# Attention over 1024-token windows: three score banks, three maxima banks, and a later place for the value matmuls

## The reference, cut to what matters

```python
x = x + _L0_conv_ref(_gn(x), L0_conv_weight)
x = x + _L1_conv_ref(_gn(x), Wr, Wqkv, Wp, bp, W1, b1, W2, b2)

def _dmha(x, Wr, Wqkv, Wp, bp):                  # inside _L1_conv_ref, x: [16, 4096 tokens, 288]
    xr = x @ Wr.T
    C2 = xr.shape[-1]                            # 144
    hd = C2 // NUM_HEADS                         # 8 heads of 18
    qkv = (xr @ Wqkv.T).reshape(B, N, 3, NUM_HEADS, hd).transpose(2, 0, 3, 1, 4)
    n = N // N_CHUNKS                            # 4 chunks of 1024 tokens
    ...
    attn = jnp.einsum('bhcnd,bhcmd->bhcnm', q, k) * scale
    attn = jax.nn.softmax(attn, axis=-1)
    o = jnp.einsum('bhcnm,bhcmd->bhcnd', attn, v)
    o = o.transpose(0, 2, 3, 1, 4).reshape(B, N, C2)
    return o @ Wp.T + bp
```

## Time and profile before

| | |
|---|---|
| median of 3 runs | 13767.46 us (13765.76 to 13772.49) |
| profiled execution, its span | 13760.1 us |
| attention phase in it | about 4479 to 12953 us |
| PE busy over the span | 93% |
| DVE busy | 71% |
| ACT busy | 57% |
| POOL busy | 20% |
| mean granted TensorE clock | 0.969 of full speed |

### The profile page before, as it was taken

One profiled execution on the slowest core, in us unless ns is written; L12 is line 12 of the kernel. 1 busy time (PEld: TensorE's weight loads), 2 busy tenths in 40 slices (PEclk: granted clock), 3 DMA queues, 4 the chain that ended last, 5 costly groups with the idle time before them and its releaser, 6 DMA issues. The chain is left out here.

```text
span 13760.1 us, 258672 instructions
## 1 busy us (share of the span) xinstructions
PE 12819.6 (93%) x76348; PEld 5285.8 (38%) x76348; DVE 9806.3 (71%) x18034; ACT 7890.2 (57%) x14774; POOL 2684.0 (20%) x2692
## 2 busy tenths in 40 slices
PE   6999999999993799999999999999999999999899
PEld 3545544544552233333333333333333333333233
DVE  7888888888886676777777777777777777677411
ACT  4666666666663365666665666666666666566511
POOL 3445444444441000000000000000000000000144
PEclk9999999999996799999999999999999999999999
DMA  2110110101104222222222232222222222222254
GB/s 73 21 21 15 21 20 16 21 15 21 21 15 134 67 61 67 65 62 63 67 65 63 61 71 63 60 68 66 61 62 66 67 63 61 66 63 64 62 127 105
DMA packets 853449, 773.62 MB, mean 56 GB/s; under 512 B 587076, under 2 KB 621348, under 8 KB 840740
## 3 DMA queue, kind: packets, MB, share of 16 engines
q1 hardware_dynamic: 850468, 747.29, 24.0%
q10 hardware_dynamic: 1536, 8.39, 0.3%
HBM read 510.50 MB, written 244.96 MB: 55 GB/s over the span
## 5 line engine op out<-in xcount | busy, mean ns | idle before, releaser
L1495 DVE TENSOR_REDUCE a_big<-a_mp 128x1 f32<-128x512 f32 x8192 | 5225.0, 685 | 2325.0 <-PE a_mp L1328 2060.3
L1414 ACT ACTIVATE a_ex<-a_sc 128x512 f32<-128x512 f32 x8192 | 4450.3, 599 | 2366.1 <-PE a_sc L1316 2121.6
L1328 PE MATMUL a_mp<-a_ks,a_qs 108*128 108x512 bf16 x8192 | 3188.5, 389 | 188.5 <-DVE a_big L1495 86.1
L1316 PE MATMUL a_sc<-a_qs,a_ks 111*128 111x512 bf16 x8192 | 3157.0, 387 | 125.3 <-issue 80.6
L849 DVE TENSOR_TENSOR r_prod<-r_pg,r_win 128x512 f32<-128x512 f32 x3584 | 2318.9, 683 | 533.1 <-PE r_pg L583 279.6
L1342 PE MATMUL a_po<-a_ex,a_va 128*32 128x512 f32 x16384 | 2221.0, 615 | 18.6 <-ACT a_ex L1414 17.8
L1230 POOL TENSOR_TENSOR a_pieces<-a_left,a_pieces 128x512 bf16<-128x512 f32 x256 | 295.4, 1154 | 7904.8 <-ACT a_pieces L1400 7904.8
L1316 PEld LDWEIGHTS a_sc<-a_qs,a_ks 111*128 111x128 bf16 x8192 | 797.2, 98 | 2529.3 <-ACT a_ex L1414 1807.7
L524 POOL TENSOR_TENSOR r_prod<-r_temp,r_win 128x512 f32<-128x512 f32 x1024 | 1214.8, 1207 | 1401.8 <-PE r_pl L632 621.3
L1328 PEld LDWEIGHTS a_mp<-a_ks,a_qs 108*128 108x128 bf16 x8192 | 802.3, 98 | 1598.8 <-DVE a_big L1495 1009.9
L587 PE MATMUL r_pg<-r_ident,r_spread 128*128 128x128 f32 x9216 | 1195.7, 278 | 112.0 <-DVE r_prod L849 93.3
(11 more groups left out here) (192 smaller groups left out, 11692.5 us busy)
## 6 DMA issues: line engine op xcount, KB each, us to landing
a_qs<-qk_parts SPq DMA_DIRECT2D x768, 144.0 KB
a_ks<-qk_parts SPq DMA_DIRECT2D x768, 144.0 KB
qk_parts<-a_pieces SPq DMA_DIRECT2D x128, 768.0 KB, 5.0
f_t<-mixed SPq DMA_DIRECT2D x48, 1536.0 KB, 16.4
a_tw<-second SPq DMA_DIRECT2D x512, 128.0 KB, 3.0
mixed<-a_t SPq DMA_DIRECT2D x256, 256.0 KB, 2.1
r_win<-first SPq DMA_DIRECT2D x128, 280.5 KB, 5.2
a_zw<-layered SPq DMA_DIRECT2D x192, 144.0 KB, 11.8
```

The lines of the kernel that those rows point to most:

```text
L1316: pe.matmul(sc[x][:, :], ks[0:KROWS + NPART, p.h, head, 128 * kb:128 * kb + 128], qs[0:KROWS + NPART, p.h, head, CHUNK * qb:CHUNK * qb + C ...
L1328: pe.matmul(mp[half][:, :], qs[0:KROWS, p.h, head, 128 * q:128 * q + 128], ks[0:KROWS, p.h, head, CHUNK * half:CHUNK * half + CHUNK], star ...
L1414: nc.scalar.activation(ex[:, k % RING, :], sc[x][:, :], ACT.Exp, scale=scale).then_inc(exped.sem, 1)
L1495: nc.vector.tensor_reduce(big[:, x % 2, k // 2:k // 2 + 1], mp[x % 2][:, :], AX_X, ALU.max).then_inc(maxed.sem, 1)
```

## The change

The eight PSUM banks are dealt out anew: three for scores, three for maxima, one each for `po` and `pm`. Tile k of a unit, scores and maxima alike, uses bank k % 3 of its kind. A unit has 128 tiles, which is not a multiple of three, so `bank_before` works out which earlier tile used the bank last, within the unit or at the end of the unit before. The value matmuls of the step before move by one tile: they now stand after the third score and maximum of a step. On ACT, `outputs` moves behind all four exponentials of its step.

```diff
+BANKS = 3
+PER_UNIT = QUAD * STEPS
+
+
+def bank_before(k):
+
+    if k >= BANKS:
+        return k - BANKS + 1
+    return max(j for j in range(PER_UNIT - BANKS, PER_UNIT) if j % BANKS == k % BANKS) - PER_UNIT + 1
...
-    sc = [ctx.enter_context(nc.psum_tensor(f"a_sc{i}", [128, CHUNK], F32)) for i in range(QUAD)]
-    mp = [ctx.enter_context(nc.psum_tensor(f"a_mp{i}", [128, CHUNK], F32)) for i in range(2)]
+    sc = [ctx.enter_context(nc.psum_tensor(f"a_sc{i}", [128, CHUNK], F32)) for i in range(BANKS)]
+    mp = [ctx.enter_context(nc.psum_tensor(f"a_mp{i}", [128, CHUNK], F32)) for i in range(BANKS)]
...
-            if not (isinstance(p.n, int) and p.n == 0 and k < QUAD):
-                pe.wait_ge(exped.sem, exped.at(p.n, k - QUAD + 1))
-            pe.matmul(sc[x][:, :], ks[0:KROWS + NPART, p.h, head, 128 * kb:128 * kb + 128],
+            if not (isinstance(p.n, int) and p.n == 0 and k < BANKS):
+                pe.wait_ge(exped.sem, exped.at(p.n, bank_before(k)))
+            pe.matmul(sc[k % BANKS][:, :], ks[0:KROWS + NPART, p.h, head, 128 * kb:128 * kb + 128],
...
-            pe.wait_ge(maxed.sem, maxed.at(p.n, k - 1))
-            pe.matmul(mp[half][:, :], qs[0:KROWS, p.h, head, 128 * q:128 * q + 128],
+            pe.wait_ge(maxed.sem, maxed.at(p.n, bank_before(k)))
+            pe.matmul(mp[k % BANKS][:, :], qs[0:KROWS, p.h, head, 128 * q:128 * q + 128],
...
-                    if x == 1 and t == 0 and -1 in which:
+                    if x == 2 and t == 0 and -1 in which:
                         values(p.to(-1), STEPS - 1)
-                    elif x == 1 and t and 0 in which:
+                    elif x == 2 and t and 0 in which:
                         values(p, t - 1)
...
-                nc.scalar.activation(ex[:, k % RING, :], sc[x][:, :], ACT.Exp, scale=scale).then_inc(exped.sem, 1)
+                nc.scalar.activation(ex[:, k % RING, :], sc[k % BANKS][:, :], ACT.Exp, scale=scale).then_inc(exped.sem, 1)
...
                 if 0 in which:
                     exponentials(p, t, 0)
+                    exponentials(p, t, 1)
                 if t == 0 and -1 in which:
                     outputs(p.to(-1), 3)
                 elif t and t % 8 == 0 and 0 in which:
                     outputs(p, t // 8 - 1)
-                if 0 in which:
-                    exponentials(p, t, 1)
...
-            nc.vector.tensor_reduce(big[:, x % 2, k // 2:k // 2 + 1], mp[x % 2][:, :],
+            nc.vector.tensor_reduce(big[:, x % 2, k // 2:k // 2 + 1], mp[k % BANKS][:, :],
```

## The result

| | before | changed |
|---|---|---|
| median | 13769.37 us (4 runs, 13765.76 to 13772.49) | 13452.02 us (4 runs, 13439.59 to 13459.34) |
| ratio, 95% interval | | 0.9768 (0.9754 to 0.9781) |
| span of the profiled execution | 13760.1 us | 13457.6 us |

The change makes the kernel 317 us faster. The forecast was 284 us faster, 13483 us, in a range of 13435 to 13590. A control of the same kernel beside the experiments gave 13443.08 against 13763.5, 320 us less.

The account below looks back on a forecast made before the run. PE was taken as the bound, with maximum matmuls waiting for reductions to free their banks. Terms -267 - 17 + 13 - 4 - 9 = -284 us, from 13767.5 to 13483 us; 8-of-10 range 13435 to 13590.

Parts of the forecast that it names:

- steps 2 to 31 of 62 units, waits of the maxima: Attention steps where maxima wait for a bank: 4.3 us saved per unit in 62 units, -267 us.
- steps 0 and 1 of 33 units that no return precedes: Unit starts that are no loop start: 0.52 us saved at each of 33, -17 us.
- unit -1: Unit with maxima only, at half clock: 2.4 in place of 2.8 in 19 steps, plus three projection steps, -9 us.
- unit 63: Unit with scores only: values come 0.17 us sooner in some 25 steps, -4 us.
- The third maxima bank: Steps without a task: maxima no longer wait for reductions, so each step loses its 0.46 us excess and runs at 2.85.
- The margins of 0.15 and 0.24: Fed steps: the tightest maximum finds its bank free 0.15 us early, the tightest score 0.24 us early.
- the rival of half the gain: Fourth reduction comes 0.35 us later, nine steps a unit keep 0.2 to 0.25 of waiting: 13611 us, chance 0.10.
- The third maxima bank, with the later place of the values: Heading of the -267 us term, which costed the extra bank and the moved value matmuls as one item.
- One score bank less costs nothing in the steady steps: Steady steps: each score finds its bank free, 0 us; if the cover went, each 0.1 us would cost 56 us.
- Loop starts: Starts of 29 loop rounds: PE stops earlier with three score banks, 0.45 us each, +13 us, bounds 0 and 29.
- the clock's rival: Lower clock for longer at loop starts, or in the steps themselves, makes the kernel slower: chance 0.05.
- The engines did not slow each other: Answers the no-change rival: unpaused engines slow each other, reductions stretch from 0.60 to 0.8, near 13767 us; chance 0.04.
- the 250 us more: Extra gain if matmuls of fed steps stood about 131 ns apart, as the Trainium skill says, not 0.22 us.

Follow-up runs that it names:

- banks alone: Changed kernel with the value matmuls and the copy of `po` put back to their old place, three and three banks kept: 13459.23 us, ratio 0.9781.
- the score bank alone: Kernel before with three score banks in place of four, two maxima banks, eighth bank unused, old place of the values: 13773.19 us, ratio 1.0003.
- the two loops of twelve: Twelve units per loop round in place of two: changed kernel 13187.48 us, ratio 0.9579; kernel before 13507.73 us, ratio 0.9810.
- the place alone: Changed kernel's order (values behind the third tile, `po` copy behind all exponentials) with the old four score and two maxima banks: 14136.24 us, ratio 1.0269.

## Why the prediction was right, by its own steps

The sum of the prediction was -284 us, the two profiled executions differ by -302.5. Read off their traces, unit by unit:

| step of the prediction | forecast | in the trace |
|---|---|---|
| steps 2 to 31 of 62 units, waits of the maxima | -267 | -269.4 |
| steps 0 and 1 of 33 units that no return precedes | -17 | -19.8 |
| steps 0 and 1 behind the 29 returns | +13 | +13.7 (control: +1.9) |
| PE's gap at the return itself | 0 | -7.4 |
| unit 0 | 0 | -7.1 |
| unit -1 | -9 | -13.3 (control: -10.5) |
| unit 63 | -4 | -3.9 |
| other phases | 0 | +4.5 |

**The third maxima bank** was right in mechanism and size. Steps 20 to 24, 30 and 31 took 2.85. Steps 14 and 25, which the prediction also put at 2.85, have a task of their own and took 5.05 and 3.28, but they lost the same 0.46 and 0.47. The margins of 0.15 and 0.24 held, and the rival of half the gain falls with them.

**"The third maxima bank, with the later place of the values"** was a false pairing. The place gives nothing in the steady steps (banks alone: 2.84 too); it trims 16 us, mostly at the edges of units. With two banks it costs 2.7%. That the pairing did no harm to the number is luck: the same count with the old place gives 2.85 as well.

**One score bank less costs nothing in the steady steps**: right (the score bank alone). The next one would cost 791 us.

**Loop starts**: the mechanism is seen in the trace (PE stops at step 0's fourth score, one piece of 5.12 us). The size lies between 0 and 14 us and is not settled: one trace says 13.7, the control 1.9, the score bank alone 11.6, and the medians of the two loops of twelve nothing. Behind the 29 returns of one trace these two steps together vary with a standard deviation of 1.0 to 1.5 us, from which I estimate a chance error of about 10 us for such a difference of two traces. That +13.7 stands so near +13 is therefore luck.

**What was missed.** Unit 0 runs the steady form with nine such steps of its own; I left it out of the 62 and gave it nothing, and it saved 7.1. PE's gap at the return shrank from 2.94 to 2.69 us on average; it is 2.69 with the banks alone too, and 2.83 with the place alone and with the score bank alone, and no experiment says why. Unit -1 ran its steps at 2.39 as forecast, and gained 2 to 4 us more, most of it in the steps with tasks, whose lengths differ between the traces of one kernel. Lastly, the median moved by 317 and the profiled executions by 302: the span of the profiled run of before lies 9 us under the median, that of the changed kernel 6 us over. I had set the forecast by the first offset alone. Single executions of this kernel differ by up to 23 us, and those of before by up to 27; the control's span, 325 us shorter, lies 8 us under its median.

**A slip in the description.** The kernel's loop covers units 2 to 61 in 30 rounds with 29 returns, and units 0 and 1 are written out before it. The text ahead of the prediction says units 4 to 61 in 29 rounds. The count of 29 slow starts, units 4 to 60, is right, as is every term that uses it.

**The other rivals.** The granted clock of unit 21 stayed at 1.00, and the mean of the profiled run is 0.969 as before, so neither form of the clock's rival came. From unit 0 to unit 62 both traces have the lower level behind returns alone, 11.3 us of it for each before, and 10.5 (control: 11.3) after. The engines did not slow each other either: reductions take 685 ns in both pages, and three in a row still follow each other at (1.89 - 0.69)/2 = 0.60 us. Score and maximum matmuls stand 0.22 us apart in the fed steps too, the pace that the sum kept; the 250 us more, estimated from a closer one, did not come.

## What to carry to other kernels

When two engines share buffers in a ring, and the producer has a stretch in which it makes nothing for the consumer, the ring must hold what the consumer can eat in that stretch and after, and this shows as waits of the producer although both engines have time to spare. Count the depth of each ring by such a schedule of one step, from the rows, and for every kind of step: the order of work may have been fitted to the old depth, so that a new order without the new depth is worse than either. And before looking at steps, see what a loop's return costs and how often it comes.

## What was not expected of the hardware

A return of the loop costs 10.2 us by the medians with either split of the banks, and 10.2 (before) to 11.1 us (after) by the traces. In the two returns shown, ACT starts again 10.48 and 10.81 us after its last instruction, PE after 2.78 and 2.67, and DVE after 4.86 in the second. TensorE's granted clock falls to 0.50, its lower level of 1.2 GHz, after PE's own short pause, and is back for good 6.3 us (before) and 4.7 us (after) after PE works again behind ACT's. In the changed kernel it also rose to 1.00 for a while in between, from 7407.8 to 7411.1, when PE was nearly all idle. Twelve units written out one after the other show no such pause between them, so it belongs to the jump back and not to the amount of code. Why ACT's is the longest remains open.
